# Up projection as three fp32r products of high and low halves

## The reference

```python
perceived = conv_general_dilated(x, w_perc, padding='SAME', feature_group_count=C) + b_perc
hid = gelu(einsum('bphw,dp->bdhw', perceived, w_up1) + b_up1, approximate=False)
dx = einsum('bdhw,cd->bchw', hid, w_up2) + b_up2
h = x + dx
q, k, v = split(einsum('bhwc,dc->bhwd', h, w_qkv) + b_qkv, 3)
# scores of q with the zero padded k of the 3 x 3 neighbours, softmax over the nine
out = h + sum_i softmax(scores)_i * v_shifted_i
```

## Time and profile before

| what | us |
|---|---|
| time, median of 3 runs | 422.68 (422.41 to 423.8) |
| the profiled execution | 422.88, of which span 421.1 |

### The profile page before, as it was taken

How to read it: one execution, slowest core, us unless ns; L and a number is a source line. 1 busy time by engine, 2 the same in 40 slices (tenths; PEclk the granted TensorE clock), 3 DMA queues, 4 the chain that set the end, 5 groups by cost and what they waited for, 6 DMA issues and landing times.

```text
span 421.1 us, 9743 instructions
## 1 busy us (share of the span) xinstructions
PE 401.5 (95%) x3590; PEld 344.7 (82%) x3590; DVE 323.3 (77%) x635; ACT 272.3 (65%) x650; POOL 168.0 (40%) x154
## 2 busy tenths in 40 slices
PE   2799989999999999999999999999999999999895
PEld 1698786979889797988879798888979798897674
DVE  4987679786878878686887868688696868774666
ACT  6532558577566758766666867756685775765673
POOL 6926254451526344152534425253533515310100
PEclk9979999999999999999999999999999999999999
DMA  7320303013050401304040220404031020300003
GB/s 250 129 64 1 114 2 112 2 37 129 3 163 0 142 22 42 120 0 162 0 162 0 77 85 0 162 0 162 0 120 42 14 87 0 102 15 36 2 16 136
DMA packets 11366, 28.54 MB, mean 68 GB/s; under 512 B 2384, under 2 KB 3024, under 8 KB 11344
## 3 DMA queue, kind: packets, MB, share of 16 engines
q1 hardware_dynamic: 10496, 28.20, 19.8%
q10 hardware_dynamic: 848, 0.05, 0.1%
HBM read 19.85 MB, written 8.39 MB: 67 GB/s over the span
## 4 chain that ended last, share of the span: by engine, by line
PE 87%; DVE 8%; ACT 2%; issue 1%; ACTq 1%; POOL 0%; DVEq 0%
PE m_ps L431 45%; PE work L444 12%; PE s_ps L497 9%; PE work L450 7%; PE work L455 7%; PE s_ps L480 5%; PE s_ps L472 1%; DVE wlo L783 1%; DVE y L853 1%; DVE y L856 1%; DVE s_ps L801 1%; DVE ptc L908 1%; ACT hid L614 1%; DVE y L852 0%; DVE pt L923 0%
## 5 line engine op out<-in xcount | busy, mean ns | idle before, releaser
L431 PE MATMUL m_ps<-thi,whi 128*128 128x248 f32 (+1 forms) x576 | 175.9, 305 | 2.3 <-DVE wlo L783 2.3
L431 PE MATMUL m_ps<-thi,wlo 128*128 128x248 f32 (+1 forms) x576 | 161.8, 281 | 0.0
L431 PE MATMUL m_ps<-tlo,whi 128*128 128x248 f32 (+1 forms) x576 | 160.4, 278 | 0.0
L431 PEld LDWEIGHTS m_ps<-thi,whi 128*128 128x128 f32 x576 | 109.6, 190 | 11.9 <-issue 8.1
L431 PEld LDWEIGHTS m_ps<-tlo,whi 128*128 128x128 f32 x576 | 110.6, 192 | 7.2 <-issue 7.2
L431 PEld LDWEIGHTS m_ps<-thi,wlo 128*128 128x128 f32 x576 | 109.6, 190 | 0.0
L1063 POOL TENSOR_TENSOR p_sb<-p_sb,rsum 128x384 f32<-128x384 f32 x32 | 27.9, 870 | 160.2 <-DVE rsum L897 160.2
L1056 POOL TENSOR_TENSOR tlo<-t,thi 128x1024 fp32r<-128x1024 f32 (+1 forms) x32 | 60.4, 1912 | 58.8 <-ACT thi L598 58.8
L614 ACT ACTIVATE hid<-y,b1eff 128x1024 f32<-128x1024 f32 x31 | 35.6, 1149 | 66.6 <-DVE y L866 43.9
L659 ACT COPY pt<-ptc 32x256 f32<-32x256 f32 (+3 forms) x189 | 74.0, 392 | 6.0 <-DVE ptc L908 1.4
L444 PE MATMUL work<-hid,w2T 128*128 128x512 f32 x120 | 54.1, 594 | 2.3 <-ACT hid L614 2.3
(11 more groups left out here) (116 smaller groups left out, 603.6 us busy)
## 6 DMA issues: line engine op xcount, KB each, us to landing
xp<-x_planes SPq DMA_DIRECT2D x16, 640.0 KB, 5.6
xr<-x_rows SPq DMA_DIRECT2D x16, 512.0 KB, 4.2
out<-o_sb SPq DMA_DIRECT2D x28, 256.0 KB, 4.2
out<-y SPq DMA_DIRECT2D x4, 256.0 KB, 2.1
w1T<-w SPq DMA_DIRECT2D x1, 384.0 KB, 3.2
w2T<-w SPq DMA_DIRECT2D x1, 128.0 KB, 4.5
wqk_in<-w_qk SPq DMA_DIRECT2D x1, 128.0 KB, 4.3
mask_bf<-masks SPq DMA_DIRECT2D x1, 120.0 KB, 4.2
```

What stands on the lines that cost most here:

```text
L431: last = pe.matmul(m_ps[:, b, col + first:col + end], a[:, j, dy, half * P:(half + 1) * P], c[:, par, T_PLACE[j], first + by:end + by], st ...
```

## The change

- **PE.** `up` is written as three fp32r products, `w2hi*hid_hi`, `w2lo*hid_hi` and `w2hi*hid_lo`: 12 matmuls of 512 columns in place of 4 in fp32. It stands behind units 4 and 5 instead of ahead of them; units 6 and 7 follow it, then the wait for `h_done`; unit 8 stands where unit 6 did, and units 9 to 11 follow the scores. `last_attention` is unchanged.
- **ACT.** New `high_hid`: `hid_hi` is `hid` as fp32r, 1024 columns for each half; for half 1 of image n-1 behind `take_m13`, for half 0 of image n behind `take_q`. `gelu` of half 0 stands ahead of `take_q`. One cast of the weights in the start-up.
- **POOL.** New `low_hid`: `hid_lo`, 1024 columns for each half. `differences` now makes `fc` and `ge` of image n+2, in the middle of body n, and waits for `transform` of image n+1 to have read the old ones; the two sums of `ab` are `sums_ab`, still for image n+1. `low_t` stays on POOL for images 0 to 2.
- **DVE.** `low_t` from image 3 on. `combine_y` stands ahead of `add_h`, and `finish_y` ahead of `sum_h`.

```diff
@@ -434,16 +442,28 @@
                 if col:
                     last.then_inc(m_ready, 1)
 
-            def up(n, c):
-
-                pe.wait_ge(hid_done, n * 2)
+            def up(n):
+
+
+                def add(c, w, half, h, **kw):
+                    return pe.matmul(up_bank(n, c), w[:, half * C:(half + 1) * C], h[:, half, c * CH:(c + 1) * CH], **kw)
+
+                pe.wait_ge(hhi_done, n * 2 - 1)
+                pe.wait_ge(hlo_done, n * 2 - 1)
                 if from_image(n, 2):
 
                     pe.wait_ge(z_done, n * 4 - 4)
-                for half in range(2):
-                    last = pe.matmul(up_bank(n, c), w2T[:, half * C:(half + 1) * C],
-                                     hid[:, half, c * CH:(c + 1) * CH], start=(half == 0), stop=(half == 1))
-                last.then_inc(up_ready, 1)
+                for c in range(NCH):
+                    add(c, w2hi, 0, hid_hi, start=True, stop=False)
+                    add(c, w2lo, 0, hid_hi, start=False, stop=False)
+                    add(c, w2hi, 0, hid_lo, start=False, stop=False)
+                pe.wait_ge(hhi_done, n * 2)
+                for c in range(NCH):
+                    add(c, w2hi, 1, hid_hi, start=False, stop=False)
+                    add(c, w2lo, 1, hid_hi, start=False, stop=False)
+                pe.wait_ge(hlo_done, n * 2)
+                for c in range(NCH):
+                    add(c, w2hi, 1, hid_lo, start=False, stop=True).then_inc(up_ready, 1)
 
             def project_q(n, hp, c, b):
                 cols = slice(W + c * CH, W + (c + 1) * CH)
...
@@ -557,20 +577,22 @@
                 units(0, 1, 2, 3)
                 if isinstance(n, int) and n == 1:
                     pe.wait_ge(wt_copied, 3)
+                    pe.wait_ge(w2hi_done, 1)
+                    pe.wait_ge(w2lo_done, 1)
                     pe.wait_ge(zeroed, 5)
                 if attn and from_image(n, 3):
                     for g in range(2):
                         values(n, 1 - par, g)
-                if attn:
-                    up(n, 0)
-                    up(n, 1)
                 units(4, 5)
+                if attn:
+                    up(n)
+                units(6, 7)
                 if attn:
                     pe.wait_ge(h_done, n * 2)
                     project_v(n, 1 - par, 0)
                     project_q(n, 1 - par, 0, 2)
                     project_q(n, 1 - par, 1, 0)
-                units(6)
+                units(8)
                 if attn:
 
                     pe.wait_ge(q_done, n * 2 - 1)
...
@@ -578,7 +600,7 @@
                     pe.wait_ge(q_done, n * 2)
                     project_v(n, 1 - par, 2)
                     scores(n, 1 - par)
-                units(7, 8, 9, 10, 11)
+                units(9, 10, 11)
 
             steady(pe, body, last_attention)
 
...
@@ -610,10 +632,18 @@
                     act.wait_ge(b1_done, 1)
                 if from_image(n, 1):
 
-                    act.wait_ge(up_ready, n * 2)
+                    act.wait_ge(hlo_done, n * 2 + (half - 1))
                 nc.scalar.activation(hid[:, half, :].rearrange("p (r k s) -> p k r s", k=K4, s=WIN),
                                      y[:, half, :, :].rearrange("p k (r s) -> p k r s", s=WIN), ACT.Gelu,
                                      bias=b1eff[:, half:half + 1]).then_inc(hid_done, 1)
+
+            def high_hid(n, half):
+
+                act.wait_ge(hid_done, n * 2 + (half + 1))
+                if from_image(n, 1):
+
+                    act.wait_ge(up_ready, n * 2)
+                nc.scalar.copy(hid_hi[:, half, :], hid[:, half, :]).then_inc(hhi_done, 1)
 
             def first_products(i):
 
...
@@ -689,7 +720,7 @@
                     act.wait_ge(y_part_done, B * 8)
                     act.wait_ge(y_done, B * 2 + c)
                     if c == 0:
-                        act.wait_ge(up_ready, B * 2 - 2)
+                        act.wait_ge(hlo_done, B * 2 - 2)
                     nc.scalar.activation(hid[:, 1, c * CH:(c + 1) * CH].rearrange("p (r k s) -> p k r s", k=K4, s=WIN),
                                          y[:, 1, :, c * rows:(c + 1) * rows].rearrange("p k (r s) -> p k r s", s=WIN),
                                          ACT.Gelu, bias=b1eff[:, 1:2]).then_inc(hid_done, 1)
...
@@ -717,22 +748,23 @@
                     gelu(n - 1, 1)
                 if conv:
                     take_m13(n, 0)
+                if attn:
+                    high_hid(n - 1, 1)
                 if store:
                     place_p(n, par, (0, 1))
-                t_late = isinstance(n, int) and n == 1
-                if more and not t_late:
+                if more:
                     high_t(n + 1, 1 - par)
                 if store:
                     place_p(n, par, (2, 3))
+                if conv:
+                    gelu(n, 0)
                 if isinstance(n, int) and n == 1:
                     act.wait_ge(consts_done, 2)
                 if attn:
                     for c in range(NCH):
                         take_q(n, c)
-                if t_late:
-                    high_t(n + 1, 1 - par)
-                if conv:
-                    gelu(n, 0)
+                if more:
+                    high_hid(n, 0)
                 if attn:
                     for i in range(4):
                         exp(n, i)
...
@@ -776,6 +808,13 @@
                 for j, a, by, b in ((3, f, 2.0, c), (4, f, -2.0, c), (0, g, 4.0, c), (5, f, -4.0, e)):
                     nc.vector.scalar_tensor_tensor(out=t[:, T_PLACE[j], :], in0=a, scalar=by, in1=b, op0=ALU.mult,
                                                    op1=ALU.add).then_inc(td_done, 1)
+
+            def low_t(n, par):
+
+                for i, part in enumerate(T_PARTS):
+                    dve.wait_ge(thi_done, n * 2 + (i + 1))
+                    nc.vector.tensor_tensor(tlo[:, par, part, :], t[:, part, :], thi[:, par, part, :].bitcast(F32),
+                                            ALU.subtract).then_inc(tlo_done, 1)
 
             def low_weights(j, k):
 
...
@@ -981,22 +1022,21 @@
 
                 if more:
                     transform_ab(n + 1, 1 - par)
-                if isinstance(n, int) and n == 0:
+                if conv:
                     combine(n, 0)
-                if from_image(n, 1) and conv:
-                    combine(n, 0)
-                if isinstance(n, int) and n == 1:
-                    sum_h(n, par)
                 if more:
                     transform(n + 1, 1 - par)
+                if conv:
+                    combine_y(n, 0)
                 if attn and from_image(n, 3):
                     for g in range(2):
                         add_h(n, 1 - par, g)
-                if from_image(n, 2) and attn:
+                if conv:
+                    finish_y(n, 0)
+                if attn:
                     sum_h(n, par)
-                if conv:
-                    combine_y(n, 0)
-                    finish_y(n, 0)
+                if more and from_image(n, 2):
+                    low_t(n + 1, 1 - par)
                 if attn:
                     for part in range(3):
                         take_v(n, 1 - par, part)
...
@@ -1045,6 +1085,8 @@
                                         ALU.subtract).then_inc(fcge_done, 1)
                 nc.gpsimd.tensor_tensor(rows(ge[:, 0, :]), plane(3, -1), plane(1), ALU.subtract).then_inc(fcge_done, 1)
                 nc.gpsimd.tensor_tensor(rows(ge[:, 1, :]), plane(0, 1), plane(2), ALU.subtract).then_inc(fcge_done, 1)
+
+            def sums_ab(n):
                 pool.wait_ge(ab_done, n * 2 + 2)
                 nc.gpsimd.tensor_tensor(t[:, T_PLACE[1], :], ab[:, 0, :], ab[:, 1, :], ALU.add).then_inc(tp_done, 1)
                 nc.gpsimd.tensor_tensor(t[:, T_PLACE[2], :], ab[:, 0, :], ab[:, 1, :],
...
@@ -1056,6 +1098,14 @@
                 nc.gpsimd.tensor_tensor(tlo[:, par, part, :], t[:, part, :], thi[:, par, part, :].bitcast(F32),
                                         ALU.subtract).then_inc(tlo_done, 1)
 
+            def low_hid(n, half):
+                pool.wait_ge(hhi_done, n * 2 + (half + 1))
+                if from_image(n, 1):
+
+                    pool.wait_ge(up_ready, n * 2)
+                nc.gpsimd.tensor_tensor(hid_lo[:, half, :], hid[:, half, :], hid_hi[:, half, :].bitcast(F32),
+                                        ALU.subtract).then_inc(hlo_done, 1)
+
             def normalise(n, g):
 
                 tiles = slice(4 * g, 4 * g + 4)
...
@@ -1065,20 +1115,28 @@
                                         ALU.mult).then_inc(pn_done, 1)
 
             differences(0, 0)
+            sums_ab(0)
             pool.wait_ge(whi_done, 1)
             pool.wait_ge(end0_done, 1)
             nc.gpsimd.tensor_tensor(wlo[:, 0, :, :], end0, whi[:, 0, :, :].bitcast(F32),
                                     ALU.subtract).then_inc(wlo_done, 1)
             for i in range(len(T_PARTS)):
                 low_t(0, 0, i)
```

(25 more changed lines are left out.)

3 lines of the change are left out of this document (added).

## The result

The changed kernel took 497.72 us (median of 4 runs, 496.96 to 499.11), beside 422.56 for the kernel before in the same rounds. The ratio is 1.1785, 95% interval 1.1764 to 1.1806: clearly slower. The profiled execution has a span of 497.3 us, 76.2 more than the 421.1 of before.

The account below looks back on a forecast made before the run. The prediction took PE to bound the kernel, hiding a ring through DVE by only 0.3 us. Span 421.1 plus 52 for the waits, 24 for the clock and 1.8 around the span gave 499 us; range 468 to 514.

Parts of the forecast that it names:

- PE's part: `up` on PE: 12 fp32r matmuls take 2.8 us instead of 3.43; gain 0.6 us a body if PE stays the bound.
- Rival D: fp32r products miss the unit's rate: `up` takes 5.1 us instead of 3.4, swallowed by idle PE, still 499; no chance given.
- The ring: Waits from scores through ACT, DVE, POOL and `project_v` to the next scores: 4.3 us longer, 28.5 us a body.
- The first `t` operation: DVE's `transform` beside `hid_lo`: its first operation is held to end at +3.7 instead of +1.8, 2.0 us lost.
- The rule on the shared port: Each POOL operation locks out one DVE operation with two SBUF operands to its end; `transform` is held like `combine_y`.
- Rivals B: Only one hold bites, as `low_hid` starts behind `transform`: a body loses 2.2 us, time 449; chance 0.10.
- C: PE stays the bound, DVE not held as said: 419 to 424, or about 414 with a shorter ring; chance 0.14.
- The clock: PE's clock falls in the idle time before `project_v`: 2.0 us in 12 bodies, 24 us, bounds 0 and 38.
- Rival A: The ring lengthens as forecast but PE's clock stays up: 475 us; chance 0.21.
- The bodies that differ: Bodies 1 to 4, 14, 15 and the tail get their own sizes; with 38.7 for bodies 5 to 13, 52 us.
- Body 1: +5 us: `high_hid` ahead of the second `take_m13` (1.05), `low_hid` holding `combine_y` (1 to 2) and `transform` (2).
- The tail: The end of the kernel starts 1.0 us earlier against its scores.

Follow-up runs that it names:

- the kernel with PE kept busy: Changed kernel plus twelve fp32r matmuls, result unread, ahead of PE's wait for `h_done` from image 2 on; 477.16 us, ratio 1.1293.
- last experiment: Kernel with `sum_h`, `take_q`, `transform` and `take_m13` moved earlier, plus `take_m13` of half 1 ahead of `high_hid` in body 0; 416.16 us, ratio 0.9858.
- half of `hid_lo`: Changed kernel with POOL subtracting only 512 of the 1024 columns of `hid_lo` of half 1, from image 1 on; 465.73 us, ratio 1.1023.
- both with the differences back: Changed kernel with `differences` again for n+1 at the start of POOL's body, 497.03 us; the same plus twelve unread fp32r matmuls on PE, 469.71 us.
- transform first: Changed kernel with DVE's `transform` moved ahead of `transform_ab` and `combine` from image 1 on; 468.15 us, ratio 1.1078.

## Why the prediction was right, step by step

The forecast was 499 us and the measurement 497.72; the mechanism is the one forecast, and most terms held. That the two lie so near is partly luck. By the legs from `project_v` 0 to the scores, the low clock cost 26.1 us in bodies 2 to 13 (predicted 24) and 1.3 in the tail (predicted 0), 27.4 together; the rest of the 76.2 is 48.8, where the prediction had 52. The two errors nearly cancel.

- **PE's part.** The twelve matmuls take 2.75 us in the trace (0.23 apart), predicted 2.8. Rival D is out.
- **The ring.** From the end of `take_m13` (242.36) the last `sum_h` operation ends at +11.4, predicted +11.6. The first `t` operation was held as predicted. Three `y` operations of half 0 were held as predicted, by the three operations named. From the first `row_max` to the end of `take_m13` it is 10.56 us (before 12.21, so 1.65 given back; predicted 1.6). From `project_v` to `row_max` it is 6.29 at full clock, taken from the kernel with PE kept busy. From the same point, the start of the first matmul (189.80 in the timeline before), it was 6.18: the six matmuls took 0.94 behind a wait instead of 0.83, which stood in no term. Together 28.3, predicted 28.5.
- **The rule on the shared port.** The trace had never shown `transform` beside POOL. It is held like `combine_y`: the pair took 2.63 us beside a `hid_lo` of 2.41, and 1.53 beside one of 1.30. The Trainium skill (SBUF — State Buffer, SBUF: two separate sides) states the exclusive lock for such operations; the traces agree. Rivals B and C fall with it: the `t` operation and three `y` operations were held, in each loop body (the pair at 2.62 to 2.65 us in each).
- **The clock.** The term was 2.0 us a body, with 0 and 3.2 as bounds; it measured 2.45 in the loop. It is the term that was too small. The fall came some 2.2 us into the idle time, not 0.9, so 5.1 us of the leg ran at the lower level and not 3.5. Rival A (475) is answered by the kernel with PE kept busy: 28.30 against 30.75.
- **The bodies that differ.** Here sizes were off, both ways, and cancelled. The steps are by the first `row_max` operations, the clock's 2.0 spread over bodies 2 to 13 as the prediction did:

```
                    predicted    measured
start to body 1        +5.0        +5.0
body 2                 +3.7        +5.0
body 3                 +5.0        +4.2
body 4                 +5.0        +2.5
bodies 5 to 13        +56.7       +58.2
body 14                +2.0        +1.9
body 15                -0.6        -0.7
tail                   -1.0        +0.1
sum                     76          76
```

  In body 4 no low clock is to be seen in the leg: its idle time was 2.94 us. Bodies 5 to 13 hold both errors: the ring took 4.1 us a body instead of 4.3 (36.6 for 38.7), the clock 21.6 for 18.
- **Body 1** came out at +5.0, but one of its parts was wrong: `high_hid` ahead of `take_m13` (1.05) costs nothing, since POOL's queue ends later (last experiment). By the timelines `take_m13` of body 1 starts 2.1 us later (41.64 against 39.54), which is the hold of the last `combine_y` operation of body 0. From there to `project_v` 0 it is 8.6 us against 5.8. The hold of `transform` is 2.0 of these 2.8 (2.79 us for the pair against 0.76). The rest was in no term: `transform`, `combine_y` and `finish_y` now stand ahead of `sum_h` in body 1, and didn't before.
- **The tail** didn't start 1.0 earlier against its scores. Timeline of PE in the changed kernel, the last `up`, and before:
```profile
473.44 3.29 PE L532 MATMUL m_ps<-hid,w2T 128*128 128x512 f32 x4 [2.16 <-ACT hid L724]
```
```profile
398.48 1.98 PE L512 MATMUL m_ps<-hid,w2T 128*128 128x512 f32 x4 [1.27 <-ACT hid L693]
```
  The idle time is longer by 0.9 and the clock, 0.99 in 472 to 474, was 0.50 in 474 to 476: 1.3 us more for the four matmuls. The prediction put the clock's price on bodies 2 to 13 only. In the three such kernels in which the clock stayed up there (half of `hid_lo`, and both with the differences back) the tail did come 1.2 us earlier, so that term was right and the clock took it back.

## What to carry to other kernels

Before giving a bound engine less work by giving others more, follow the ring that runs beside it, from the point where it is released to the point where it is waited for, and read its slack; here it was 0.1 to 0.3 us a body, and an edit that saved PE 0.6 cost 6.5. GpSimd work beside VectorE operations with two SBUF operands counts on VectorE with most of its length (here 4.1 of 5.7 us: `hid_lo`, `fc`, `ge` and `ge` against what the held operations took beyond their 0.75 and 0.41), so the steps that somebody waits for go ahead of it: the same work in another order gave 416.6 instead of 497.7 us. And a wait on TensorE has two prices, its own length and the clock behind it, of which the second may come or go with a fraction of a microsecond of the first.

## What the runs showed of the hardware that I had not expected

How long PE idles decides only in part whether the clock falls. The gap ahead of `project_v` 0, and how often its six matmuls then ran at the lower level (1.66 us instead of 0.94 in the timelines), in the bodies where the gap had its steady length:

```
kernel                           gap us        bodies   first products at 1.2 GHz
transform first                  2.60 - 2.62      9      3
half of hid_lo of half 1         2.74 - 2.78      9      1
differences put back             2.92 - 2.95     10      9
the change as made               3.86 - 3.87      9      8
```

One of the gaps, in PE's timeline of the kernel with `transform` first:
```profile
213.82 1.64 PE L475 MATMUL work<-wvT,h_around 128*128 128x129 f32 x6 [2.61 <-DVE h_around L1016]
```
The next body, with a gap of 2.62, ran the same products in 0.94. The table counts falls ahead of these products only. In the one body left of the change as made, and in the one left with the differences put back, the clock fell 1.3 and 1.0 us after PE had resumed; with half of `hid_lo` it did so in bodies 3 and 4, behind gaps of only 1.89 and 1.84 us. The last `up` shows it best: its gap is 2.16 or 2.17 us in eight kernels, and the clock fell during the four matmuls behind it in five of them and stayed at 1.00 in three. The Trainium skill (TensorE: Matmul & The Clock Gate, Part 1) has an idle engine fall to the half rate; the nine gaps of 3.9 us agree with it, each with a fall in it or just behind it, while most gaps of 2.6 and 2.8 us left the clock up. What else decides (where the gap lies in time is one candidate) is not settled by these runs. Nor is the price of a fall fixed: 2.45 us a body in the change as made, 2.99 with the differences put back, where the gap was shorter.
